# First attention's main units: division by the sums of exp moved from the probabilities to the product with V

## The reference

```
attn = einsum('bqc,bkc->bqk', q * scale, k) + rel_h + rel_w     # 196 keys per window
attn = softmax(attn, axis=-1)
out  = einsum('bqk,bkc->bqc', attn, v)
out  = out @ proj_w + proj_b                                    # then x = shortcut + out
```

## Time and profile before

| | |
|---|---|
| median of 3 runs | 886.08 us (885.78 to 888.82) |
| profiled execution | 884.12 us, its span 882.3 us |
| mean granted TensorE clock | 0.95 |
| PE busy | 789.6 us, 89% |
| PEld busy | 644.7 us, 73% |
| DVE busy | 513.7 us, 58% |
| ACT busy | 433.0 us, 49% |
| POOL busy | 143.4 us, 16% |
| chain that ended last | PE 70%, SP's queue 11%, DVE 7%, issue 4%, POOL 3%, DMA 2%, ACT 2% |

### The profile page before, as it was taken

The page is one execution under the profiler, slowest core; times in us unless marked ns, Lnnn a source line. Parts: engine busy times, 40 slices in busy tenths (PEclk is TensorE's granted clock), DMA queues, the critical chain, the costliest instruction groups (busy, mean ns, idle before and its releaser), DMA issues.

```text
span 882.3 us, 20283 instructions
## 1 busy us (share of the span) xinstructions
PE 789.6 (89%) x6794; PEld 644.7 (73%) x6794; DVE 513.7 (58%) x1516; ACT 433.0 (49%) x1419; POOL 143.4 (16%) x293
## 2 busy tenths in 40 slices
PE   3688798897988887789998999999999999997998
PEld 2566576675756654589986888888888888876998
DVE  5156657667576677455525475756575666674542
ACT  1035445556465565454424465555555555554432
POOL 8310111102011110032221011010101010100211
PEclk9569889999899999799996999999999999999999
DMA  6482010100101010100030303030303030300001
GB/s 94 99 197 41 6 35 9 28 21 16 27 7 34 11 26 2 36 1 1 0 57 17 58 16 70 5 74 1 74 0 71 0 71 1 74 1 1 19 18 36
DMA packets 39950, 29.89 MB, mean 34 GB/s; under 512 B 13382, under 2 KB 38038, under 8 KB 39872
## 3 DMA queue, kind: packets, MB, share of 16 engines
q1 hardware_dynamic: 36518, 26.16, 14.0%
q0 software_dynamic: 2544, 2.35, 1.6%
q10 hardware_dynamic: 810, 0.40, 0.3%
HBM read 8.79 MB, written 1.57 MB: 12 GB/s over the span
## 4 chain that ended last, share of the span: by engine, by line
PE 70%; SPq 11%; DVE 7%; issue 4%; POOL 3%; DMA 2%; ACT 2%; DVEq 0%; POOLq 0%; ACTq 0%
PE bank L1236 10%; PE bank L1315 8%; PE bank L495 7%; PE bank L474 7%; SPq L1129 6%; PE bank L1263 5%; PE bank L1243 5%; PE bank L1282 4%; PE bank L1104 3%; PE bank L920 3%; PE bank L1343 3%; PE bank L937 3%; PE bank L1375 3%; PE bank L1038 2%; SPq L1593 2%
## 5 line engine op out<-in xcount | busy, mean ns | idle before, releaser
L666 ACT ACTIVATE Pb<-bank,nmax 128x256 f32<-128x256 f32 (+1 forms) x432 | 192.3, 453 | 95.7 <-DVE nmax L656 93.0
L656 DVE TENSOR_REDUCE nmax<-bank 128x2 f32<-128x392 f32 (+2 forms) x240 | 139.0, 580 | 51.1 <-PE bank L1236 30.2
L677 DVE TENSOR_SCALAR Pb<-Pb,rsum 128x196 f32<-128x196 f32 (+2 forms) x432 | 133.7, 347 | 8.5
L696 ACT COPY area<-bank 98x392 f32<-98x392 f32 (+1 forms) x144 | 77.4, 539 | 82.9 <-PE bank L1243 71.0
L1236 PE MATMUL bank<-K,Q 80*128 80x256 f32 x384 | 107.4, 405 | 5.5 <-DMA Q<-rel_dense 5.5
L1236 PEld LDWEIGHTS bank<-K,Q 80*128 80x128 f32 x384 | 69.4, 198 | 25.2 <-issue 14.5
L666 ACT ACTIVATION_READ_ACCUMULATOR Pb<-bank,nmax 128x1 f32 x432 | 87.4, 202 | 0.0
L937 PE MATMUL bank<-ident,Pb 128*98 128x128 f32 x384 | 65.2, 296 | 22.7 <-DVE Pb L677 22.7
L484 ACT ACTIVATE area<-bank,fc1b 128x256 f32<-128x256 f32 x96 | 45.2, 475 | 66.0 <-PE bank L474 64.8
L937 PEld LDWEIGHTS bank<-ident,Pb 128*98 128x98 f32 x384 | 42.3, 135 | 37.4 <-DVE Pb L677 17.6
L495 PE MATMUL bank<-fc2w,area 128*128 128x192 f32 x384 | 64.7, 326 | 0.0
(11 more groups left out here) (143 smaller groups left out, 1542.2 us busy)
## 6 DMA issues: line engine op xcount, KB each, us to landing
Q<-dense_q SPq DMA_DIRECT2D x16, 288.0 KB, 4.7
K<-dense_k SPq DMA_DIRECT2D x16, 288.0 KB, 6.7
operands<-dense_q SPq DMA_DIRECT2D x48, 32.0 KB, 2.0
operands<-dense_k SPq DMA_DIRECT2D x48, 32.0 KB, 2.0
Q<-rel_dense SPq DMA_DIRECT2D x32, 48.0 KB, 2.6
Q<-rel_dense POOLq DMA_DIRECT2D x32, 48.0 KB, 2.4
out<-x_all SPq DMA_DIRECT2D x8, 192.0 KB, 2.0
operands<-dense_q SPq DMA_DIRECT2D x45, 28.0 KB
```

Of the source, the lines that this page charges most:

```text
L656: nc.vector.tensor_reduce(nmax[0:sc.shape[0], u % 3, 0:sc.shape[1]], sc, AX.X, ALU.max, negate=True).then_inc(self.m_rdy, 1)
L666: nc.scalar.activation(Pb[u % 3][0:rows, t, 0:cols], sc[:, t, :], ACT.Exp, bias=nmax[0:rows, u % 3, t:t + 1], accum_out=esum[0:rows, u % 3 ...
L677: nc.vector.tensor_scalar(Pb[u % 3][0:rows, t, 0:keep], Pb[u % 3][0:rows, t, 0:keep], rsum[0:rows, u % 3, t:t + 1], None, ALU.mult).then_i ...
L696: copy(*self.pt_views(u)).then_inc(self.pt[self.pt_engine(u)], 1)
```

## The change

Main units of `a0` are no longer normalised before the transposition; rem units (`normed_first`) are as before. For a main unit exp is written without `accum_out`, there is no reciprocal and no multiplication of `Pb`, and the transposition waits for exp alone. V's tiles get a column of ones at channel 16 of each head (the tile of the big window only), so the product with V leaves each head's sums of exp at partition 32j+16 of `O_BANK`. After the copy into `AO0` a new product (`pe_sums`) with the constant `pick_sum`, a 128 x 128 matrix of zeros and ones, spreads each head's row of sums over the head's 32 partitions, into columns 256 to 451 of `O_BANK`; `dve_divide` takes the reciprocal of these 128 x 196 sums and multiplies `AO0` by it. The three small copies of `act_ao` go to DVE behind the large one. `pe_sums` and `dve_divide` for a group are in slots 7, 13 and 1, one after its values; the previous image's projection and `dve_back` move from slot 1 to slot 2 (`BACK_AT`). In the second attention nothing is changed in what is executed.

```diff
             def act_exp(self, eng, n, u):
...
                 for t in range(k):
+                    total = esum[0:rows, u % 3, t:t + 1] if self.normed_first(u) else None
                     nc.scalar.activation(Pb[u % 3][0:rows, t, 0:cols], sc[:, t, :], ACT.Exp,
-                                         bias=nmax[0:rows, u % 3, t:t + 1],
-                                         accum_out=esum[0:rows, u % 3, t:t + 1]).then_inc(self.e_rdy, 1)
+                                         bias=nmax[0:rows, u % 3, t:t + 1], accum_out=total).then_inc(self.e_rdy, 1)
             def dve_norm(self, eng, n, u):
+                if not self.normed_first(u):
+                    return
...
             def pe_slot(self, eng, n, u, has_prev, ahead):
...
                 if u == 2 and ahead(self.NU - 1, 1):
                     self.pe_transpose_x(eng, n.next())
+                for m, g in self.sums_at(n, u, has_prev):
+                    self.pe_sums(eng, m, g)
                 for m, g in self.groups_at(n, u, has_prev):
                     self.pe_values(eng, m, g)
-                if u == self.VALUES_BEHIND and has_prev:
+                if u == self.BACK_AT and has_prev:
                     self.pe_back(eng, n.prev())
             def dve_slot(self, eng, n, u, has_prev, ahead):
...
                 if ahead(u, 3):
                     self.dve_max(eng, *ahead(u, 3))
+                for m, g in self.sums_at(n, u, has_prev):
+                    self.dve_divide(eng, m, g)
                 for m, g in self.groups_at(n, u, has_prev):
                     self.dve_ao(eng, m, g)
                 if u == 1 and ahead(self.NU - 1, 1):
                     self.dve_xhat(eng, n.next())
-                if u == self.VALUES_BEHIND and has_prev:
+                if u == self.BACK_AT and has_prev:
                     self.dve_back(eng, n.prev())
...
         class Attention0(Attention):
+            BACK_AT = 2
+            def normed_first(self, u):
+                return self.units[u][0] == "rem"
             def act_ao(self, eng, n, q):
+                pass
+
+            def dve_ao(self, eng, n, q):
                 eng.wait_ge(self.pv, n.at(3, q + 1))
...
+                nc.vector.tensor_copy(ao[:, 0:WS, 0:WS], O_BANK[:, 0:N0].rearrange("p (r c) -> p r c", c=WS))\
+                  .then_inc(self.raw, 1)
                 for dst, at, k in parts:
-                    nc.scalar.copy(dst, O_BANK[:, at:at + k].rearrange("p (r c) -> p r c", c=dst.shape[2]))\
+                    nc.vector.tensor_copy(dst, O_BANK[:, at:at + k].rearrange("p (r c) -> p r c", c=dst.shape[2]))\
                       .then_inc(self.ao[0], 1)
+            def sums_at(self, n, u, has_prev):
+                if u == 1:
+                    return [(n.prev(), 2)] if has_prev else []
+                return [(n, u // 6 - 1)] if u in (7, 13) else []
+            def pe_sums(self, eng, n, q):
+                eng.wait_ge(self.raw, n.at(3, q + 1))
                 eng.wait_ge(self.ao[0], n.at(9, 3 * q + 3))
+                if n.counts(3, q):
+                    eng.wait_ge(self.ao[1], n.at(3, q))
+                nc.tensor.matmul(O_BANK[:, T:T + N0], pick_sum[:], self.ao_view(q)[:, 0:WS, 0:WS],
+                                 start=True, stop=True).then_inc(self.sums, 1)
+            def dve_divide(self, eng, n, q):
+                eng.wait_ge(self.sums, n.at(3, q + 1))
+                nc.vector.reciprocal(over_sum[:], O_BANK[:, T:T + N0]).then_inc(self.inverse, 1)
+                eng.wait_ge(self.inverse, n.at(3, q + 1))
+                nc.vector.tensor_tensor(self.ao_view(q)[:, 0:WS, 0:WS], self.ao_view(q)[:, 0:WS, 0:WS],
+                                        over_sum[:].rearrange("p (r c) -> p r c", c=WS),
+                                        ALU.mult).then_inc(self.ao[1], 1)
...
+            nc.vector.tensor_copy(pick_sum[:].rearrange("p (j m) -> p j m", j=4),
+                                  ident[:].rearrange("p (j m) -> p j m", j=4)[:, :, D0:D0 + 1].broadcast_to([P, 4, 32]))\
+              .then_inc(pick_done, 1)
...
-                for z in zero_v:
-                    nc.gpsimd.memset(z[:], 0.0).then_inc(zeroed_v, 1)
+                for i in range(2):
+                    nc.gpsimd.memset(VR0[i][:, :, D0:32], 0.0).then_inc(zeroed_v, 1)
+                    nc.gpsimd.memset(V0[i][:, :, :, D0 + 1:32], 0.0).then_inc(zeroed_v, 1)
+                    nc.gpsimd.memset(V0[i][:, :, :, D0:D0 + 1], 1.0).then_inc(zeroed_v, 1)
```

More of the change, by code:

```diff
@@ L200, in build @@
                   sb("reltab_h1", [CH, 31]), sb("reltab_w1", [CH, 31])]
+        pick_sum = sb("pick_sum", [P, P])
+        over_sum = sb("over_sum", [P, N0])
         blk0 = sb("blk0", [CH, GH0])
@@ L287, in build @@
         kpad_done = sem("kpad_done")
+        pick_done = sem("pick_done")
         obias_done = sem("obias_done")
@@ L622, in __init__ @@
                                for e in range(2)]
+                self.norm_cum = [sum(self.normed_first(v) for v in range(u)) for u in range(self.NU + 1)]
                 s = f"a{l}_"
@@ L647, in pe_scores @@
                     mm.then_inc(self.s_rdy, 1)
+            def normed_first(self, u):
+                return True
             def score_tiles(self, u):
@@ L674, in dve_norm @@
                 nc.vector.reciprocal(rsum[0:rows, u % 3, 0:k], esum[0:rows, u % 3, 0:k]).then_inc(self.r_rdy, 1)
-                eng.wait_ge(self.r_rdy, n.at(self.NU, u + 1))
+                eng.wait_ge(self.r_rdy, n.at(self.norm_cum[-1], self.norm_cum[u + 1]))
                 for t in range(k):
@@ L680, in pe_probsT @@
             def pe_probsT(self, eng, n, u):
-                eng.wait_ge(self.p_rdy, n.at(self.NTL, self.cum[u + 1]))
+                if self.normed_first(u):
+                    done = self.norm_cum[u + 1] * len(self.tiles(u))
+                    eng.wait_ge(self.p_rdy, n.at(self.norm_cum[-1] * len(self.tiles(u)), done))
+                else:
+                    eng.wait_ge(self.e_rdy, n.at(self.NTL, self.cum[u + 1]))
                 m, v = (n, u - 2) if u >= 2 else (n.prev(), self.NU + u - 2)
@@ L809, in step @@
                             self.pe_values(eng, n, last)
+                            self.pe_last_sums(eng, n, last)
                             self.pe_back(eng, n)
@@ L814, in step, with pe_last_sums, dve_last_divide @@
                             self.dve_ao(eng, n, last)
+                            self.dve_last_divide(eng, n, last)
                             self.dve_back(eng, n)
                 image_loop(eng, step)
+            def pe_last_sums(self, eng, n, q):
+                pass
+            def dve_last_divide(self, eng, n, q):
+                pass
             def groups_at(self, n, u, has_prev):
@@ L823, in groups_at @@
                 return [(n, g) for g in self.pv_after.get(behind, ())]
+            def sums_at(self, n, u, has_prev):
+                return []
             def pe_slot(self, eng, n, u, has_prev, ahead):
@@ L984, in act_ao, with sums_at, pe_last_sums, dve_last_divide @@
                 for dst, at, k in parts:
-                    nc.scalar.copy(dst, O_BANK[:, at:at + k].rearrange("p (r c) -> p r c", c=dst.shape[2]))\
+                    nc.vector.tensor_copy(dst, O_BANK[:, at:at + k].rearrange("p (r c) -> p r c", c=dst.shape[2]))\
                       .then_inc(self.ao[0], 1)
-            def dve_ao(self, eng, n, q):
-                eng.wait_ge(self.pv, n.at(3, q + 1))
-                eng.wait_ge(self.ao[0], n.at(9, 3 * q + 3))
[L991 to L994, removed]
+            def sums_at(self, n, u, has_prev):
+                if u == 1:
+                    return [(n.prev(), 2)] if has_prev else []
+                return [(n, u // 6 - 1)] if u in (7, 13) else []
+            def pe_last_sums(self, eng, n, q):
+                self.pe_sums(eng, n, q)
+            def dve_last_divide(self, eng, n, q):
+                self.dve_divide(eng, n, q)
+            def pe_sums(self, eng, n, q):
+                eng.wait_ge(self.raw, n.at(3, q + 1))
+                eng.wait_ge(self.ao[0], n.at(9, 3 * q + 3))
+                if n.counts(3, q):
[9 more added lines that the diff above has]
+                                        ALU.mult).then_inc(self.ao[1], 1)
             def pe_back(self, eng, n):
@@ L1199, in setup @@
                 self.gath = sem("a0_gather")
+                self.raw = sem("a0_raw")
+                self.sums = sem("a0_sums")
+                self.inverse = sem("a0_inverse")
                 self.xmain = [sem("a0_xm0"), sem("a0_xm1")]
@@ L1216, in build @@
             VALUES_BEHIND = 1
+            BACK_AT = 1
             def pt_engine(self, u):
@@ L1533, in pe_meanwhile @@
             pe.wait_ge(kpad_done, 1)
+            pe.wait_ge(pick_done, 1)
             pe.wait_ge(ld_const, 16 * len(first_rows))
@@ L1674, in scatter_first @@
                 a0.scatter_rel(act, 0, range(GH0 // 2, GH0))
-                act.wait_ge(zeroed_v, 4)
```

(3 more changed lines are left out.)

1 line of the change is left out of this document (removed).

## The result

The changed kernel takes 914.3 us (median of 4 executions, 908.7 to 920.3) against 885.9 us (885.6 to 888.8): a ratio of 1.032, 95% interval 1.029 to 1.035. Timed again (experiment 12) it took 913.2 us. The forecast was 902 us in a range of 879 to 914: the direction held, the size was 28.4 us instead of 16, and the time lies just outside the range.

What follows compares the result with a forecast made beforehand. Each image was bound by SP's DMA queue, then by PE and those who release it. Six images 12.6, clock 5.1, start -0.5, last image -0.5: +16.7 on 884.12 us, 900.8; median forecast 902, range 879 to 914.

Steps and rivals of the forecast that it cites:

- the gap: Slot 2, ahead of the transposes of x: PE idles some 2.5 us waiting for DVE's xhat, in six images.
- B: An image from its first scores to the end of the second k product: 16.4 us, forecast +2.1 us in six images.
- the reciprocal: DVE's reciprocal of the 128x196 sums in dve_divide: taken as 1.3 us, from 6 ns a column.
- part A: From DVE's k copy to the next image's first scores: fixed by SP's DMA queue, stays 21.3 us.
- the clock: PE's granted clock falls in dense work after the new wait: 1.7 us each, 3 of 6 images, 5.1 us.
- rival 2: The clock falls after all six new PE waits, for one or two stretches: 908 to 918 us; chance 0.12.
- the last image: First attention, no next image: removed waits pay 5 to 6 us against added work; net -0.5 us.
- the start: POOL fills half as many elements of V before the first bias product: -0.5 us, between -1 and +0.7.
- the step from the profile to the median: Median of the changed kernel taken to lie 2.0 us over its profiled execution, as in the runs shown.
- rival 3: PE's speed counts throughout, so removed waits for Pb's multiplication pay: -9.9 us, 878 us; chance 0.17.

Runs made afterwards that it cites:

- experiment 12: The changed kernel unaltered, timed again: 913.2 us, ratio 1.029 to the kernel before.
- experiment 5: Changed kernel with five unused 192-column products on PE ahead of the transposes of x in slot 2: 911.7 us, ratio 1.026.
- experiment 3: Changed kernel with the 128x196 reciprocal replaced by a copy of the same shape: 897.1 us, ratio 1.014.
- experiment 6: Changed kernel with half of the bias DMAs issued by POOL instead of SP: 903.1 us, ratio 1.017.
- 7: Kernel before the change with the same half of the bias DMAs issued by POOL: 884.0 us, ratio 0.995.
- experiment 4: Changed kernel with dve_xhat ahead of dve_divide, and projection and dve_back in slot 3: 897.2 us, ratio 1.014.
- experiment 8: Changed kernel with next image's statistics before dve_ao, dve_xhat before dve_divide, projection and dve_back in slot 3, half the bias DMAs on POOL: 878.2 us, ratio 0.989.

## Why the prediction was right or wrong

**Right, nearly to the tenth: the gap.** xhat ended 312.44, 10.0 us after the first scores; the prediction's 296.0 less 285.95 is 10.05. PE idled 2.0 to 2.2 us ahead of the transposes in all six images (forecast 2.5), for the cause that was named, and `dve_back` held `dve_xn` back as described (0.23 to 0.31 us at the q product in five of the six, forecast 0.2). B without a fall is then 1.8 us longer (experiment 5), where the sum had 2.1.

**Right: the reciprocal,** taken as 1.3 us. These are the groups of the changed kernel by line and shape:

```profile
L1049 DVE RECIPROCAL over_sum<-bank 128x196 f32<-128x196 f32 x24 | 32.9, 1373 | 1.1 <-PE bank L1044 1.1
...
L1044 PE MATMUL bank<-area,pick_sum 128*128 128x196 f32 x48 | 13.6, 365 | 4.2 <-issue 2.8 <-DVE area L1018 1.4
...
L1051 DVE TENSOR_TENSOR area<-area,over_sum 128x196 f32<-128x196 f32 x24 | 8.7, 363 | 0.8
...
L1023 DVE COPY area<-bank 128x28 f32<-128x28 f32 x48 | 6.5, 177 | 0.0
```

1373 ns against 149 for one column are 6.3 ns a column, the 6 of rows 6. That a difference of one column carried to 196 held so well is partly luck, as the prediction itself called it a short lever; experiment 3 shows that the 1.0 us over a copy is on the path. The Trainium skill's repeat count of 8 ("VectorE: DVE Perf Modes", First, the fixed hardware budget), read as eight times a plain column, had given about 1.8 us; the trace shows an operation that costs 3.8 times a copy of the same shape (363 ns), so that reading gives too much.

**Right: part A.** It is 20.9 to 22.3 us in the six images (forecast 21.3), with the granted clock at 1.00 throughout. It follows the time of SP's 24 issues: 20.9 us where they took 17.0 together, 21.1 to 21.4 with 17.5 to 17.7, and 22.0 and 22.3 with 18.3 and 18.7. The DMA wait at its end grew as forecast, and experiments 6 and 7 show that SP's queue sets it after the change.

**Wrong in size: the clock.** The step that failed is "I put a fall into 3 of 6 images: 5.1 us". It fell behind every one of the six gaps, in both profiles of the changed kernel, so the term is 10.2 us; the price of one, 1.7 us, was right (1.6 in experiment 5). B grew by 20.8 + 20.7 + 21.8 + 19.6 + 19.8 + 19.8 - (17.6 + 16.7 + 16.5 + 17.2 + 16.4 + 16.4) = 21.6 us (unrounded), where the forecast had 12.6 + 5.1 = 17.7 and with all six 22.8. This was rival 2's case, which had a chance of 0.12 and of which the range left out half: its 908 to 918 us hold the median, and the profiled execution's +24.6 lies in the lower part of its +21.8 to +32. A gave 2.2 us back: the kernel before had two falls of 6.8 us there, at 117.7 and 233.8 us (A 22.9 us each time, granted clock 0.85), the changed kernel had none.

**Wrong in sign: the last image.** "Net -0.5 us" became +3.1. The removed waits were to pay 5 to 6 us, and PE's waits for the multiplication did fall by 4.8, from 7.3 to 2.5. But 2.4 us of waits for copies and exp came in their place, which the sum had not; `pe_sums` and the projection wait 3.0 us longer, and PE is busy 2.2 us longer. The end cost more than 2.2 (timeline of the changed kernel):

```profile
382.79 0.36 DVE L1018 COPY area<-bank 128x196 f32<-128x196 f32 x1 [2.06 <-PE bank L1000]
...
383.51 0.99 PE L1044 MATMUL bank<-area,pick_sum 128*128 128x196 f32 x2 [0.79 <-DVE area L1018]
384.54 1.38 DVE L1049 RECIPROCAL over_sum<-bank 128x196 f32<-128x196 f32 x1 [1.13 <-PE bank L1044]
...
386.42 4.18 PE L1062 MATMUL bank<-wproj,area 128*128 128x192 f32 x12 [1.92 <-issue]
```

From the large copy's start to the projection it is 3.6 us; before it was 0.9 from the first of ACT's copies, so 2.7 more.

**Wrong: the start and the step from the profile to the median.** The start was to give 0.5 us and cost 1.5: SP issued its first bias and q DMAs at 73.2 instead of 71.6 us, because the loads of the later stages' weights ahead of them in its queue took longer. That is scatter for the most part: the first such DMA goes out at 71.6 to 73.3 us in the four profiles without the change and at 71.4 to 74.4 in the ten with it. And the median of the changed kernel lies 5.6 us over its profiled execution, not 2.0 (3.2 in experiment 12). Together: 16.7 + 3.9 (B) - 2.2 (A) + 3.6 (last image) + 2.0 (start) + 0.7 (other stages) = 24.7 us of the profiled execution, and 3.6 more in the median.

One sum of the recorded text is off: rival 3's -9.9 us gives 876 us by its own way from profile to median, not 878.

## What to carry to other kernels

When an instruction is moved in an engine's order, ask what it was covering: here a projection of 2.2 us stood exactly where PE would otherwise have waited, and moving it by one slot alone brings two thirds of the loss or more. A saving on a path that is as long as a DMA queue's beside it brings nothing until the queue is shortened too; the same change cost 28 us as it was made, and it saved some 8 us with the queue split and the gap closed. And if a new gap of 2 us stands ahead of dense matmuls, reckon with the fall of the clock behind nearly every one of them, as it came here in 17 of 18, and not behind half.

## What the runs showed of the hardware

Behind the gaps of 2.0 to 2.2 us ahead of the transposes of x the granted clock fell to the 1.2 GHz level in all twelve cases of the two profiles of the changed kernel, and in five of six in experiment 6. Behind the shorter gap in the same place it fell in three of six cases (0.98 to 1.16 us, experiment 3) and in none of six (0.84 to 1.02 us, experiment 4). The length of the gap does not decide it alone: in the two profiles of the changed kernel PE waits 1.6 to 3.1 us for DMAs ahead of the first scores of the third to the eighth image, and the clock fell behind three of these twelve waits only. What parts the two places was not found. And in the kernel before it fell twice without any gap, at 117.7 and 233.8 us, in the middle of the second bias product, with PE busy without a pause from 110.9 and from 227.0 us on.

The unchanged stages behind the first attention took from 515.6 us (before) to 531.5 us (experiment 8) with the same instructions. Of these 15.9 us PE was busy for 9.2, at a granted clock of 0.96 instead of 0.98; it also waited 7.6 us for DMAs and 3.6 us for exp in the second attention, where before it waited 5.5 us for DMAs and not for exp. This scatter between executions is as large as many effects that one wants to measure, and a stage's own end time is the safer measure for a change inside it.
